# The scan input of a Mamba block made on GpSimd from broadcast rows, with the exponentials in PSUM

## What is computed

```python
delta = softplus(x @ wd1.T @ wd2.T + wd2_b)      # (token, 512)
Bm, Cm = x @ wB.T, x @ wC.T                      # (token, 16)
h = exp(d_l[:, :, None] * A) * h + (d_l * x_l)[:, :, None] * b_l[:, None, :]
y_l = einsum('ben,bn->be', h, c_l)
```

## Time and profile before

| | |
|---|---|
| time, median of 3 runs | 1483.13 us (1481.66 to 1486.64) |
| span of the profiled execution | 1480.3 us |
| TensorE busy | 1279.1 us |
| VectorE busy | 1243.6 us |
| ScalarE busy | 915.7 us |
| GpSimd busy | 868.9 us |
| mean granted TensorE clock | 0.930 |

### The profile page before, as it was taken

One profiled execution on the slowest core, in us unless ns is written; L12 is line 12 of the kernel. 1 busy time (PEld: TensorE's weight loads), 2 busy tenths in 40 slices (PEclk: granted clock), 3 DMA queues, 4 the chain that ended last, 5 costly groups with the idle time before them and its releaser, 6 DMA issues.

```text
span 1480.3 us, 24598 instructions
## 1 busy us (share of the span) xinstructions
PE 1279.1 (86%) x7476; PEld 1028.4 (69%) x7476; DVE 1243.6 (84%) x2066; ACT 915.7 (62%) x2017; POOL 868.9 (59%) x1284
## 2 busy tenths in 40 slices
PE   4686674999999999999999999999999999865765
PEld 3575553777778777777778777777878777754654
DVE  6787876889797888889797888889797898999996
ACT  3776676576675757566675757566575756755330
POOL 0332477766668585766758585666758545335563
PEclk8797877999999999999999999999999999976876
DMA  9400826000000000001000000001000100144232
GB/s 316 144 2 0 291 97 211 17 25 24 29 23 30 29 23 22 29 23 30 26 26 30 30 22 23 26 26 30 23 29 30 30 23 15 49 133 133 74 112 84
DMA packets 76093, 86.43 MB, mean 58 GB/s; under 512 B 9920, under 2 KB 67136, under 8 KB 75968
## 3 DMA queue, kind: packets, MB, share of 16 engines
q1 hardware_dynamic: 69536, 68.02, 14.4%
q0 software_dynamic: 6144, 16.79, 3.8%
q10 hardware_dynamic: 288, 0.07, 0.0%
HBM read 49.46 MB, written 35.39 MB: 57 GB/s over the span
## 4 chain that ended last, share of the span: by engine, by line
PE 65%; DVE 21%; issue 6%; ACT 3%; POOL 2%; DMA 1%; DVEq 0%; POOLq 0%; SPq 0%; ACTq 0%
PE bps L818 12%; PE hps L827 11%; DVE hb L1058 9%; PE bankH L941 8%; PE bankX L971 8%; PE bankV L963 8%; PE bankG L850 3%; DVE yac L1072 3%; PE bankG L948 2%; PE bankG L860 2%; PE bankV L903 2%; PE bankG L863 2%; PE bankH L903 2%; PE bankV L850 1%; DVE tok L1255 1%
## 5 line engine op out<-in xcount | busy, mean ns | idle before, releaser
L1058 DVE TENSOR_TENSOR_SCAN hb<-aexp,carry,bps 128x256 f32<-128x256 f32 x768 | 509.8, 726 | 89.8 <-PE bps L818 71.5
L515 ACT ACTIVATE aexp<-delta,Am 128x256 f32<-128x256 f32 x1024 | 440.0, 503 | 60.9 <-DVE hb L1058 54.9
L1072 DVE SCALAR_TENSOR_TENSOR yac<-hps,BC,yac 128x512 f32<-128x512 f32 x480 | 334.7, 738 | 27.6 <-PE hps L827 27.4
L818 PE MATMUL bps<-idn,ub 128*128 128x128 f32 x2048 | 298.4, 290 | 62.7 <-DVE hb L1058 44.7
L827 PE MATMUL hps<-idn,hb 128*128 128x128 f32 x2048 | 292.1, 288 | 49.2 <-DVE yac L1072 44.7
L827 PEld LDWEIGHTS hps<-idn,hb 128*128 128x128 f32 x2048 | 250.6, 149 | 101.1 <-issue 79.0
L713 POOL TENSOR_SCALAR ub<-uT,BC 128x512 f32<-128x512 f32 x448 | 312.6, 710 | 11.8 <-ACT uT L602 10.5
L818 PEld LDWEIGHTS bps<-idn,ub 128*128 128x128 f32 x2048 | 250.3, 149 | 99.4 <-issue 59.5
L799 POOL COPY carry<-hb 128x4 f32<-128x4 f32 x256 | 55.7, 218 | 232.8 <-DVE hb L1058 231.2
L1058 DVE TENSOR_TENSOR_SCAN hb<-aexp,bps 128x256 f32<-128x256 f32 x256 | 154.6, 666 | 41.6 <-PE bps L818 37.9
L775 POOL TENSOR_TENSOR vs<-g,vs 128x512 f32<-128x512 f32 x72 | 91.9, 1276 | 166.2 <-ACT vs L665 165.3
(11 more groups left out here) (172 smaller groups left out, 1812.2 us busy)
## 6 DMA issues: line engine op xcount, KB each, us to landing
xbuf<-gT SPq DMA_DIRECT2D x8, 1152.0 KB, 11.0
tok<-xbuf SPq DMA_DIRECT2D x72, 128.0 KB, 2.2
ybuf<-tok SPq DMA_DIRECT2D x72, 128.0 KB, 1.7
w<-in_W SPq DMA_DIRECT2D x2, 4096.0 KB, 24.0
xch<-in_x SPq DMA_DIRECT2D x16, 256.0 KB, 2.9
w<-in_x SPq DMA_DIRECT2D x4, 1024.0 KB, 11.1
v<-in_V SPq DMA_DIRECT2D x1, 4096.0 KB, 15.9
tok<-in_x SPq DMA_DIRECT2D x32, 128.0 KB, 2.2
```

Source lines behind the costliest of these rows:

```text
L515: nc.scalar.activation(aexp[:, u % 2, e, :], delta[:, c % 2, e, :], ACT.Exp, scale=Am[:, e, n:n + 1]).then_inc(s_a, 1)
L818: mm = pe.transpose(bps[q][:, i * CH + s * P:i * CH + (s + 1) * P], ub[:, u % 2, s, e * P:(e + 1) * P], idn[:, :])
L1058: v.tensor_tensor_scan(hb[:, u % 2, e, :], aexp[:, u % 2, e, :], bps[e // 2][:, (e % 2) * CH:(e % 2 + 1) * CH], first, ALU.mult, ALU.add). ...
L1072: ins = v.scalar_tensor_tensor(out=yac[:, c % 2, s, :], in0=hps[s][:, :], scalar=scale, in1=yac[:, c % 2, s, :], op0=ALU.mult, op1=ALU.add)
```

## The change

The addend u*B is made e-major at once, so that nothing has to be turned:

- B5 becomes: TensorE turns the 16 columns of B (two transposes), ScalarE copies the result to `brow` (16 rows of 256, in a part of `tqB`), SyncE writes it to DRAM (`brows`). For every step SyncE then loads one row, broadcast to all 128 partitions, into one of the 8 buffers of `bbc` (256 loads of 128 KB, issued up to 7 steps ahead; `load_row`, `row_loads`). B5 moves from behind U to right behind B3, and the pieces after it keep their places.
- `products(u)` is one tensor_tensor on GpSimd, 128x1024, both inputs in SBUF. It waits for the row, and for scans(u-2), which free its output buffer. For seven steps of chunk 1 (`DVE_PRODUCTS`) VectorE does it, between the scans and the pieces.
- `turn_products` goes, and with it `bps`; ScalarE writes the exponentials to these two PSUM banks (`aps`). `aexp` goes. Each bank holds the exponentials of two channel groups of one step, so that the first pair of step u+1 waits for the second scan of step u, and the second pair for the fourth. The scans read `aps` and `ub`.
- On ScalarE exps(u+1) moves from ahead of place 2n to behind it.
- `uT` goes; `ub` holds e-major data; U writes `ue` and not `xc`.

```diff
-B_PIECES = [... ("B3",), ("B4",), ("SP",), ("DL",), ("U",), ("B5",)]
+B_PIECES = [... ("B3",), ("B5",), ("B4",), ("SP",), ("DL",), ("U",)]
-    "other": [5, 7, 8, 9, 9, 10, 12, 14, 15, 18, 21, 23, 24, 26, 29],
+    "other": [5, 7, 8, 9, 9, 10, 12, 14, 15, 18, 20, 21, 23, 24, 26],
-ACT_PRODUCTS = {1: 2, 14: 2}
+DVE_PRODUCTS = {1: (1, 3, 5, 7, 9, 11, 13)}
+BROWS = 8
...
+def row_loads(c, n):
+
+    if n + BROWS - 1 < N:
+        return [N * c + n + BROWS - 1]
+    first = {13: (0, 1), 14: (2, 3), 15: (4, 5, 6)}.get(n, ())
+    return [N * (c + 1) + k for k in first] if c + 1 < CHUNKS else []
...
+            def load_row(u):
+
+                if u >= BROWS:
+                    wait_product(sp, u - BROWS)
+                if u % N == 0:
+                    sp.wait_ge(brow_w, 16 * (u // N + 1))
+                sp.dma_start(bbc[:, u % BROWS, :], brow_d[u:u + 1, :].to_broadcast([P, CH])).then_inc(ld_bb[u % BROWS], 16)
...
+                elif kind == "B5":
+                    c = piece[2]
+                    wait_taken(sp, "G", piece)
+                    sp.dma_start(brow_d[N * c:N * (c + 1), :], brow).then_inc(brow_w, 16)
...
                 for e in range(KE):
-                    at_least(act, s_scan, 4 * (u - 2) + e + 1)
-                    nc.scalar.activation(aexp[:, u % 2, e, :], delta[:, c % 2, e, :], ACT.Exp,
+                    if e % 2 == 0:
+                        at_least(act, s_scan, 4 * (u - 1) + e + 2)
+                    nc.scalar.activation(aps[e // 2][:, (e % 2) * CH:(e % 2 + 1) * CH], delta[:, c % 2, e, :], ACT.Exp,
                                          scale=Am[:, e, n:n + 1]).then_inc(s_a, 1)
...
                 for n in range(N):
+                    for piece in at[2 * n]:
+                        do(piece)
                     if N * c + n + 1 < N * CHUNKS:
                         exps(N * c + n + 1)
-                    for piece in at[2 * n] + at[2 * n + 1]:
+                    for piece in at[2 * n + 1]:
                         do(piece)
...
                 if n == 0:
-                    wait_taken(pool, "V", ("B5", 0, c))
-                at_least(pool, s_bT, 2 * (u - 1))
-                for s in range(SUB - ACT_PRODUCTS.get(c, 0)):
-                    nc.gpsimd.tensor_scalar(ub[:, u % 2, s, :], uT[:, c % 2, s, :], BC[:, c % 2, s, n:n + 1], 1.0,
-                                            ALU.mult, ALU.mult).then_inc(s_ub, 1)
+                    pool.wait_ge(uu, c + 1)
+                pool.wait_ge(ld_bb[u % BROWS], 16 * (u // BROWS + 1))
+                at_least(pool, s_scan, 4 * (u - 1))
+                nc.gpsimd.tensor_tensor(ub[:, u % 2, :, :], ue[:, c % 2, :, :],
+                                        bbc[:, u % BROWS, :].unsqueeze(1).to_broadcast([P, KE, CH]), ALU.mult).then_inc(s_ub, 1)
...
-            def turn_products(u):
...
                 elif kind == "B5":
                     c = piece[2]
-                    pe.wait_ge(uu, c + 1)
-                    for s, b in enumerate("HV"):
-                        wait_free(pe, b, piece)
-                        for e in range(KE):
-                            mm = pe.transpose(bank[b][:, e * P:(e + 1) * P], xc[:, e, s * P:(s + 1) * P], idn[:, :])
-                        mm.then_inc(full[b], 1)
+                    wait_free(pe, "G", piece)
+                    wait_taken(pe, "G", ("B3", 0, c))
+                    for s in range(SUB):
+                        mm = pe.transpose(bank["G"][0:N, s * P:(s + 1) * P], BC[:, c % 2, s, 0:N], idn[:, :])
+                    mm.then_inc(full["G"], 1)
...
-                    turn_products(u)
...
                 for e in range(KE):
-                    dve.wait_ge(s_a, 4 * u + e + 1)
                     if e % 2 == 0:
-                        dve.wait_ge(s_bT, 2 * u + e // 2 + 1)
+                        dve.wait_ge(s_a, 4 * u + e + 2)
+                    if e == 0:
+                        wait_product(dve, u)
                     first = 0.0 if c % CPB == 0 else carry[:, n, e:e + 1]
-                    v.tensor_tensor_scan(hb[:, u % 2, e, :], aexp[:, u % 2, e, :], bps[e // 2][:, (e % 2) * CH:(e % 2 + 1) * CH],
+                    v.tensor_tensor_scan(hb[:, u % 2, e, :], aps[e // 2][:, (e % 2) * CH:(e % 2 + 1) * CH], ub[:, u % 2, e, :],
                                          first, ALU.mult, ALU.add).then_inc(s_scan, 1)
...
                     scans(u)
+                    if on_vector(u + 1):
+                        products(u + 1)
```

More of the change, by code:

```diff
@@ L129, in prologue, with on_vector, vector_products @@
     x2 = [("X2", q, 0) for q in range(KE // 2)]
[L130 to L140 removed]
+    return [("B1", 0, 0)] + b2 + convs + x2 + [(k, 0, 0) for k in ("B3", "B5", "B4", "SP", "DL", "U")] + [("ST",)]
+def on_vector(u):
+    return u % N in DVE_PRODUCTS.get(u // N, ())
+def vector_products(u):
+    return sum(on_vector(w) for w in range(u + 1))
+def gpsimd_products(u):
+    return u + 1 - vector_products(u)
+def row_loads(c, n):
[3 more added lines that the diff above has]
+    return [N * (c + 1) + k for k in first] if c + 1 < CHUNKS else []
 def epilogue():
@@ L318, in mamba_moe @@
         s_ub = sem("s_ub")
-        s_uba = sem("s_uba")
-        s_bT = sem("s_bT")
+        s_ubd = sem("s_ubd")
+        brow_w = sem("brow_w")
+        ld_bb = [sem(f"ld_bb{i}") for i in range(BROWS)]
         s_a = sem("s_a")
@@ L481, in _ @@
             for c in range(CHUNKS):
-                for place in pieces(c):
-                    for piece in place:
+                at = pieces(c)
+                for n in range(N):
+                    for piece in at[2 * n] + at[2 * n + 1]:
                         do(piece)
+                    for u in row_loads(c, n):
+                        load_row(u)
             for piece in epilogue():
@@ L1047, in _, with products @@
             statistics(0)
+            def products(u):
+                c, n = divmod(u, N)
+                if n == 0:
+                    dve.wait_ge(uu, c + 1)
+                dve.wait_ge(ld_bb[u % BROWS], 16 * (u // BROWS + 1))
+                at_least(dve, s_scan, 4 * (u - 1))
+                v.tensor_tensor(ub[:, u % 2, :, :], ue[:, c % 2, :, :],
+                                bbc[:, u % BROWS, :].unsqueeze(1).to_broadcast([P, KE, CH]), ALU.mult).then_inc(s_ubd, 1)
             def scans(u):
```

61 lines of the change are left out of this document (24 added, 37 removed), and 6 rows, old and new, of the table B_PLACES.

## The result

| | before | after |
|---|---|---|
| time, median of 4 runs | 1483.49 us | 1616.47 us |
| ratio, 95% interval | | 1.0891 (1.0873 to 1.0909) |
| span of the profiled execution | 1480.3 us | 1614.8 us |
| prologue, to the first sum of chunk 0 | 57.7 | 61.1 |
| chunk 0 | 104.7 | 120.5 |

The change makes the kernel 9% slower. Chunk lengths are differences of the starts of each chunk's first sum, L1105 in the new kernel (L1070 in the earlier trace rows). One slip in the text on record: the stretch 683 to 767, and with it what it calls chunk 8 in its rows, is chunk 7 by these marks; nothing hangs on it. Where the 134.5 us went: 55 in chunks 2 to 12, 35 in chunks 14 and 15, 21 in chunk 1, 16 in chunk 0, 4 in chunk 13 and 3.5 in the prologue.

What follows compares the result with a forecast made beforehand. It took chunks 2 to 12 as bound by TensorE on average, with GpSimd's list bounding steps 3 to 8. Terms 44 + 3 + 8 + 5 + 12 = +72 us gave a span of 1552 and a time of 1555, range 1468 to 1598.

Steps and rivals of the forecast that it cites:

- the largest term: Chunks 2 to 12: 87.7 us each against 83.7, +44 us over the eleven (bounds -15 and +85).
- chunk 0 and the prologue: Start of the kernel: TensorE's relief against later exponentials and collisions of four convolutions, 0 us (-8 to +8).
- Transposes off TensorE: Chunks 2 to 12: 2048 transposes leave, TensorE falls from 81.8 to about 62 us a chunk and bounds nothing.
- Products on GpSimd: Every step: one 2.38 us product replaces 1.36 us of tensor_scalars; steps 3 to 8 grow by 3.5 us a chunk.
- The end of the stretch: Scan 3 to scan 8 of chunks 2 to 12, as long as GpSimd's list: 29.9 us becomes 33.4.
- Exponentials in PSUM: ScalarE's order in chunks 2 to 12: step 12 about 7.5 us, step 13 about 6.3, eleven steps 54.3 against 53.8.
- The port: VectorE instructions with two SBUF inputs collide with GpSimd, 1.0 us each: chunk 13 +3, chunk 14 +8, chunk 15 +5.
- The later one waits: Rule cited for VectorE with two SBUF inputs against a GpSimd instruction reading SBUF; one collision may cost 0 to 2.4 us.
- Chunk 1: Six GpSimd products fall between the 64 scatters, 14.3 us, some in idle time: +12 us (0 to +20).
- late rows: Rival: each product would wait for its row's DMA, needing loads of over 27 us; chance 0.01.
- Faster: Rival: TensorE was the only bound that counts; eleven chunks take 82.3 us each, time 1465; chance 0.17.
- Slower product or colliding scans: Rival: broadcast input or VectorE's scans stretch the product to 3.2 us, 91.0 us a chunk, time 1606; chance 0.09.

Runs made afterwards that it cites:

- exps_half: Changed kernel with exponentials in two SBUF buffers at their old place, and GpSimd's product, its result unused, cut to two of four channel groups: 1475.4 us.
- both_sbuf: Changed kernel with exponentials written to one SBUF buffer, so scans read both inputs from SBUF, and four row buffers instead of eight: 1970.7 us.

## Why the prediction was wrong, and where it was right

The direction was right, and the largest term within 11 us of 55; the time is 61 us over the forecast and 18 over the range. The step that failed is the price of a collision between VectorE and GpSimd: I took 1.0 us for each, and each cost what was left of a GpSimd instruction of 2.36 us and more. That is 22 of the missing us, in chunks 14 and 15. Next come chunk 0 and the prologue, taken at nothing (16 and 3.5 us missing), chunks 2 to 12 (11) and chunk 1 (9).

*Transposes off TensorE.* Right that TensorE stops bounding chunks 2 to 12; exps_half shows its relief, 3.7 us a chunk under before. TensorE's own time came out wrong: 75 us a chunk and not 62 (71 in exps_half, at 0.98 of full speed). Missed: the relief lowers TensorE's clock, from 0.85 to 0.64 in chunk 0, and there TensorE is still on the path. VectorE waited 15.6 us for turned states, 4.5 before; with the waits for turned products, which are gone, it was 11.2 before.

*Products on GpSimd.* 2.36 for 2.38 us, 33.8 for 33.4: as worked out. The end of the stretch came 0.4 us later because GpSimd's FB multiplication, which took 1.27 us before, took 1.72: it met the first X2 (773.05, 2.29 us), which had itself been held by a product. The sum had left this collision out.

*Exponentials in PSUM.* Step 12 7.6 for 7.5, step 13 6.4 for 6.3, the eleven steps outside the stretch 54.9 for 54.3. The sum for a chunk was 87.7 and it is 88.7: 11 us over the eleven. For step 13 the reading of the earlier trace rows was right: freed exponentials take 2.2 us off it. For step 12 the size was right and the reason was not, which is luck: VectorE doesn't wait for exponentials there, and with two buffers for them the step is still 7.3 us. ScalarE's pieces make it long, as read in the earlier trace rows, but through the FA gate and TensorE's turned states.

*The port.* This is the term that failed. The mechanism was named with its row, and the place too (the final sums), but I charged about twelve collisions of 1.0 us in chunk 14, less 4 us, and some in chunk 15: +8 and +5 where the chunks lost 17.4 each. The runs show 37 us over the two, all of it on the 64 final sums. The count was not far off (nine sums in chunk 14, eight in chunk 15), the price was: these 17 are 1.7 to 4.7 us over their 0.48, 2.5 on average. I took the growth of the product (1.0) for the price of a meeting. But chunk 14 had no product on GpSimd before, and chunk 15 had pairs of 0.7 us, so that a sum that now meets a product is held until the product ends, up to 5.15 us for one that met two instructions. The earlier trace rows had the price already: 2.85 us and not 0.47. The upper end for chunk 14 (+25) held it, the one for chunk 15 (+12) didn't. "The later one waits" isn't borne out by the starts in the trace: in the earlier trace rows the sum begins 0.20 us ahead of GpSimd's instruction and is the one that waits.

*Chunk 1.* +12 forecast, +21 measured. The products between the scatters were the part that I had; short ones took 7.8 off. "Behind the 8 MB of weights three rows may be a few us late" was the other, 9 us, and the place was named rightly, but priced at nothing in the sum. SyncE stood 45.4 us at the weights' wait, with the rows behind it, and then the weights' transfer held the first row for 25.8 us. I gave late rows a chance of 0.01 by the latency of a load (3.5 us here, 2.2 by the earlier trace rows) and seven steps of lead; behind a queued wait of another piece this lead is gone, and behind 8 MB the latency of a lone load doesn't hold. The measured +21 lies just over the range of the term (0 to +20).

*Chunk 0 and the prologue.* 0 forecast (-8 to +8), +15.8 measured in chunk 0: 8.2 products, the rest exponentials and clock. "TensorE's relief" had the wrong sign: the waits for TensorE rose. The prologue was forecast 1 us shorter and came out 3.4 longer; with short products it is 2.3 us shorter than before the change, but it moves by up to 3 us between runs that leave it alone, so this says little.

*The rivals.* Faster: its mechanism is real (3.7 us a chunk) and smaller than the two prices. Slower product or colliding scans: neither, though both_sbuf shows what colliding scans would have cost. Late rows: one product of the 249 waited for its row, 9.7 us, and that alone cost chunk 1 9 us.

## What to carry to other kernels

Count collisions in units of the other engine's whole instruction, for each VectorE instruction with two SBUF inputs in the stages where VectorE is full. When a load moves behind a queue that also issues waits and loads of other work, look for the longest wait in that queue and for the bytes issued behind it; the number of buffers ahead alone says nothing. Work taken off TensorE may slow what is left of it, as in chunk 0. A step that comes out as long as forecast is no proof of its reason: take the reason away and see whether the step gets shorter.
